# Reading the second input of VectorE's one-hot, bias and row-weighting instructions from PSUM instead of SBUF, in four graph passes and one attention stage of a graph network

## The reference

```python
def _hypergraph_conv(x, hei, W, b, num_nodes, num_edges):
    xw = x @ W.T
    edge_feat = b_inv[:, None] * segment_sum(xw[src], he)
    out = d_inv[:, None] * segment_sum(edge_feat[he], src)
    return out + b
...
logits = leaky_relu(s_dst[e0] + s_src[e1], 0.2)
m = segment_max(logits, e0)
ex = exp(logits - m[e0])
denom = segment_sum(ex, e0) + EPS
alpha = ex / denom[e0]
out = segment_sum(alpha[:, None] * h[e1], e0)
```

## Time and profile before

| what | value |
|---|---|
| median of 3 runs | 7260.24 us (7251.83 to 7262.59) |
| the profiled execution | 7256.75 us |
| its span | 7255.1 us |
| busy: PE, DVE, ACT, POOL | 4491.0, 2751.6, 961.2, 4754.5 us |
| POOL's gathers in s1 to s4 | from 137.9 us to 4546 us of the span |
| POOL's gathers in the attention | from 5461.3 us to 6693.3 us |

### The profile page before, as it was taken

One profiled execution on the slowest core, in us unless ns is written; L12 is line 12 of the kernel. 1 busy time (PEld: TensorE's weight loads), 2 busy tenths in 40 slices (PEclk: granted clock), 3 DMA queues, 4 the chain that ended last, 5 costly groups with the idle time before them and its releaser, 6 DMA issues. The chain is left out here.

```text
span 7255.1 us, 78015 instructions
## 1 busy us (share of the span) xinstructions
PE 4491.0 (62%) x18874; PEld 3567.0 (49%) x18874; DVE 2751.6 (38%) x7375; ACT 961.2 (13%) x2757; POOL 4754.5 (66%) x4610
## 2 busy tenths in 40 slices
PE   4565554666666555555556555899843656666589
PEld 3444443544554444444344444799632444444377
DVE  3111111222222111111454454322556666666644
ACT  2000000000111000000000000433330000000333
POOL 2777776777776777777777777111137777777455
PEclk8777777888888777877787888999876777777699
DMA  5888887333333333333444444052044444444445
GB/s 140 115 113 112 111 114 117 113 111 111 113 114 107 108 114 111 113 114 113 130 138 139 137 139 139 23 158 64 3 133 122 123 122 122 122 123 111 137 88 89
DMA packets 485564, 820.77 MB, mean 113 GB/s; under 512 B 108460, under 2 KB 344101, under 8 KB 485101
## 3 DMA queue, kind: packets, MB, share of 16 engines
q0 software_dynamic: 223760, 583.20, 36.2%
q1 hardware_dynamic: 261436, 232.51, 10.4%
q10 hardware_dynamic: 200, 3.43, 0.1%
HBM read 649.02 MB, written 170.02 MB: 113 GB/s over the span
## 5 line engine op out<-in xcount | busy, mean ns | idle before, releaser
L301 POOL DMA_INDIRECT s_rows<-table,ids x3328 | 3337.3, 1003 | 1111.3 <-issue 967.9
L554 PE MATMUL s_part<-s_rows,s_onehot 128*128 128x257 f32 x6656 | 2213.2, 498 | 1802.7 <-DMA s_rows<-table,ids 1774.3
L554 PEld LDWEIGHTS s_part<-s_rows,s_onehot 128*128 128x128 f32 x6656 | 1643.1, 256 | 2278.5 <-issue 1586.5
L1414 POOL DMA_INDIRECT at_rows<-h_t,ids x832 | 978.8, 1176 | 303.9 <-issue 252.0
L399 DVE TENSOR_SCALAR s_inv<-s_raw 128x1 f32<-128x1 f32 x416 | 64.0, 154 | 2857.7 <-ACT s_raw L348 2857.7
L1795 PE MATMUL at_part<-at_rows,at_onehot 128*128 128x264 f32 x1664 | 582.4, 484 | 4.9 <-DVE at_onehot L1622 4.9
L442 DVE TENSOR_TENSOR s_onehot<-iota,rel 128x1024 f32<-128x1024 f32 x416 | 510.5, 1228 | 63.6 <-DVE s_row L437 28.6
L348 ACT ACTIVATE s_raw<-s_part 128x257 f32<-128x257 f32 x416 | 161.0, 387 | 2443.3 <-PE s_part L554 2113.0
L1030 POOL COPY acc<-h 128x125 f32 x160 | 66.9, 418 | 557.7 <-DVE h L1058 557.7
L1795 PEld LDWEIGHTS at_part<-at_rows,at_onehot 128*128 128x128 f32 x1664 | 364.6, 237 | 70.8 <-issue 4.2
L2221 POOL DMA_INDIRECT out<-ex_y,ex_ids x112 | 181.1, 1617 | 162.2 <-DMA out<-ex_y,ex_ids 108.7
(11 more groups left out here) (355 smaller groups left out, 5612.6 us busy)
## 6 DMA issues: line engine op xcount, KB each, us to landing
s_rows<-table,ids POOLq DMA_INDIRECT x3328, 2.8
xs_d<-blank SPq DMA_DIRECT2D x38, 1032.0 KB, 12.7
table<-s_x SPq DMA_DIRECT2D x208, 128.0 KB, 2.6
ex_x<-xs_d SPq DMA_DIRECT2D x60, 258.0 KB, 3.3
table<-s_y SPq DMA_DIRECT2D x104, 128.0 KB, 1.9
s_at_node<-in_x SPq DMA_DIRECT2D x104, 128.0 KB, 2.8
s_at_node<-xn_d SPq DMA_DIRECT2D x104, 128.0 KB, 3.0
x_d<-s_x SPq DMA_DIRECT2D x104, 128.0 KB, 1.9
```

The source lines that it names most:

```text
L301: pool.indirect_dma_start(rows[:, t % RT, 0:D], None, table[0:NP_, :], bass.IndirectOffsetOnAxis(cst["ids"][:, t:t + 1], 0)).then_inc(rows ...
L554: ins = pe.matmul(part[u][:, 0:D + 1], onehot[:, u, t % JT, :], rows[:, t, 0:D + 1], start=False, stop=(t == JT * u + JT - 1))
L1414: pool.indirect_dma_start(rows[:, t % AHEAD, :], None, table, bass.IndirectOffsetOnAxis(cst["ids"][:, t:t + 1], 0)).then_inc(rows_in[t % A ...
```

## The change

Each stage gets one more PSUM bank (a second one in the attention), and a DVE copy at its start puts the column numbers there, and in the passes the bias behind them. The one-hots then read `iota` from PSUM and `rel` from SBUF; L410 reads `raw` from SBUF and the bias from PSUM. So that s2's banks suffice, its two `psY` become one, and `make` waits for one copy more.

In the attention the turned weights get a bank of their own, `ps_w`, and the row weighting reads them from there. That bank is single, so the weights of a round may be turned only when DVE has weighted the last tiles of the round before: the turn moves from step TIT + 2 to TIT + 5, with a wait on `weighted`, and the copy of the weights into the rows (still needed by PE, which sums them) moves from TIT + 3 to TIT + 6, with a semaphore of its own, `w_out`, on which DVE now waits at step 8.

```diff
+        fixed = m.ps(f"{name}_fixed", [P, 512])
+        iota = fixed[:, 0:P]
+        if bias is not None:
+            bias_row, bias = bias, fixed[:, P:P + D]
...
-            psY = [m.ps(f"{name}_psY{b}", [P, 512]) for b in range(2)]
+            psY = m.ps(f"{name}_psY", [P, 512])
...
+            dve.tensor_copy(iota, cst["iota"][:]).then_inc(held, 1)
+            if bias is not None:
+                dve.tensor_copy(bias, bias_row[:]).then_inc(held, 1)
+            dve.wait_ge(held, 1 if bias is None else 2)
...
-                link(dve.scalar_tensor_tensor(out=x[b][:], in0=raw[u][:, 0:D], scalar=inv[:, 0:1], in1=bias[:],
+                link(dve.scalar_tensor_tensor(out=x[b][:], in0=raw[u][:, 0:D], scalar=inv[:, 0:1], in1=bias,
...
-                dve.tensor_tensor(onehot[:, u % OG], cst["iota"][:].unsqueeze(1).to_broadcast([P, JT, P]),
+                dve.tensor_tensor(onehot[:, u % OG], iota.unsqueeze(1).to_broadcast([P, JT, P]),
...
-                pe.wait_ge(made_out, g + 1)
+                pe.wait_ge(made_out, g + 2)
...
+        ps_w = m.ps("at_ps_w", [P, 512])
+        iota = m.ps("at_iota", [P, 512])[:, 0:P]
...
+                if step == TIT + 6:
+                    act.wait_ge(w_turned, n + 1)
+                    act.sem_inc(issue, 1)
                     act.activation(rows[:, TIT * u:TIT * (u + 1), D:W],
-                                   ps_z[:, EXP:EXP + P].rearrange("p (t h) -> p t h", h=H8), ACT.Copy
-                                   ).then_inc(ex_ready, 1)
+                                   ps_w[:, 0:P].rearrange("p (t h) -> p t h", h=H8), ACT.Copy).then_inc(w_out, 1)
...
-                                      rv[:, :, D:W].unsqueeze(3).to_broadcast([P, G4, H8, D // H8]),
+                                      ps_w[:, t * H8:(t + G4) * H8].rearrange("p (t h) -> p t h", h=H8).unsqueeze(3)
+                                      .to_broadcast([P, G4, H8, D // H8]),
...
-                            dve.wait_ge(ex_ready, 3 * n + 7)
+                            dve.wait_ge(w_out, n + 2)
                             weigh_and_place(n + 1, (u + 1) % RB, t + JT - TIT)
...
-                    pe.transpose(ps_z[:, EXP:EXP + P], w[:], cst["ident"][:])
...
+                if step == TIT + 5:
+                    if not (isinstance(n, int) and n == 0):
+                        pe.wait_ge(weighted, TIT * n)
+                        pe.sem_inc(issue, 1)
+                        pe.wait_ge(w_out, n)
+                    pe.transpose(ps_w[:, 0:P], w[:], cst["ident"][:]).then_inc(w_turned, 1)
...
+                        if t == 0:
+                            pe.wait_ge(w_out, n + 1)
```

More of the change, by code:

```diff
@@ L240, in stage_row_pass @@
         summed, group_done, raw_ready = m.sem(f"{name}_summed"), m.sem(f"{name}_group_done"), m.sem(f"{name}_raw_ready")
+        held = m.sem(f"{name}_held")
         onehot_ready, cleared = m.sem(f"{name}_onehot_ready"), m.sem(f"{name}_cleared")
@@ L329, in copy_made @@
                 act.sem_inc(issue, 1)
-                act.activation(y[b][:], psY[b][:, 0:D], ACT.Copy).then_inc(made_out, 1)
+                act.activation(y[b][:], psY[:, 0:D], ACT.Copy).then_inc(made_out, 1)
             def round_of(i, opening):
@@ L374, in count_starts @@
                 dve.wait_ge(deg_turned, 2)
-                dve.tensor_copy(total[:], psY[0][:, 0:NB]).then_inc(deg_v, 1)
+                dve.tensor_copy(total[:], psY[:, 0:NB]).then_inc(deg_v, 1)
                 dve.wait_ge(deg_v, 3)
@@ L383, in count_starts @@
                 dve.wait_ge(deg_v, 6)
-                dve.tensor_tensor(cst["start"][:], upto[:], psY[1][:, 0:NB], ALU.add).then_inc(deg_v, 1)
+                dve.tensor_tensor(cst["start"][:], upto[:], psT[1][:, 0:NB], ALU.add).then_inc(deg_v, 1)
             def finish(g, u):
@@ L510, in count_starts @@
                 pe.wait_ge(deg_v, 1)
-                pe.matmul(psY[0][:, 0:NB], cst["ones"][:], deg[:], start=True, stop=True)
-                pe.matmul(psY[1][:, 0:NB], cst["before"][:], deg[:], start=True, stop=True).then_inc(deg_turned, 1)
+                pe.matmul(psY[:, 0:NB], cst["ones"][:], deg[:], start=True, stop=True)
+                pe.matmul(psT[1][:, 0:NB], cst["before"][:], deg[:], start=True, stop=True).then_inc(deg_turned, 1)
                 pe.wait_ge(deg_v, 7)
@@ L524, in make @@
                 pe.wait_ge(turned_out, g + 3)
-                pe.wait_ge(made_out, g + 1)
+                pe.wait_ge(made_out, g + 2)
                 for k in range(2):
-                    ins = pe.matmul(psY[b][:, 0:D], turned_x[b][:, k, :], w[:, k, :], start=(k == 0), stop=(k == 1))
+                    ins = pe.matmul(psY[:, 0:D], turned_x[b][:, k, :], w[:, k, :], start=(k == 0), stop=(k == 1))
                 ins.then_inc(made, 1)
@@ L1300, in stage_attention @@
         ps_line = m.ps("at_ps_line", [1, 2, 2, P])
-        EXP, INIT, FADE = P, 2 * P, 2 * P + 2
+        ps_w = m.ps("at_ps_w", [P, 512])
+        iota = m.ps("at_iota", [P, 512])[:, 0:P]
+        INIT, FADE = P, P + 2
         heads_in, node_in, starts_in = (m.sem(f"at_{n}") for n in ("heads_in", "node_in", "starts_in"))
@@ L1310, in stage_attention @@
         exped, ex_ready = m.sem("at_exped"), m.sem("at_ex_ready")
+        w_turned, w_out, held = m.sem("at_w_turned"), m.sem("at_w_out"), m.sem("at_held")
         prepared = m.sem("at_prepared")
@@ L1520, in _ @@
             fill()
+            dve.tensor_copy(iota, cst["iota"][:]).then_inc(held, 1)
+            dve.wait_ge(held, 1)
             dve.memset(carry[1][:], -BIG).then_inc(v, 1)
@@ L1610, in program @@
                     dve.wait_ge(added, 2)
-                dve.wait_ge(ex_ready, 4)
+                dve.wait_ge(w_out, 1)
                 def weigh_and_place(n, u, t):
@@ L1621, in weigh_and_place @@
                     rel = cst["rel"][:, int(not alone), :]
-                    dve.tensor_tensor(onehot[:, t:t + G4, :], cst["iota"][:].unsqueeze(1).to_broadcast([P, G4, P]),
+                    dve.tensor_tensor(onehot[:, t:t + G4, :], iota.unsqueeze(1).to_broadcast([P, G4, P]),
                                       rel[:, bass.ds(TIT * n + t, G4)].unsqueeze(2).to_broadcast([P, G4, P]),
@@ L1638, in collect @@
                         if left:
+                            dve.wait_ge(ex_ready, 2 * n + 5)
+                            dve.sem_inc(finishing, 1)
                             fades = factor[:, (u + 1) % RB, 2:2 + H8]
@@ L1659, in add_alone @@
                     if t == 0:
+                        dve.wait_ge(ex_ready, 2 * n + 3)
                         dve.wait_ge(added, TIT * n + 2)
@@ L1733, in prepare @@
                     pe.wait_ge(zc_ready, n + 1)
-                    pe.wait_ge(ex_ready, 3 * n + 1)
+                    pe.wait_ge(ex_ready, 2 * n + 1)
                     pe.transpose(ps_z[:, 0:P], zc[:], cst["ident"][:]).then_inc(pe_turned, 1)
```

## The result

The changed kernel takes **6942.69 us** (median of 4 runs, 6937.43 to 6949.73) where the kernel before takes 7258.40 on the same chip (4 runs): a ratio of 0.9566, 95% interval 0.9550 to 0.9583. The forecast of 6955 lies 12 us above it. The profiled execution took 6938.84 us, its span 6937.3, 317.8 us less than the span of before.

What follows compares the result with a forecast made beforehand. POOL's own gather rate was taken to bound passes and attention. 337.6 us removed, less 32 given back and 4 for the tie, gave 302 us: 7256.75 becomes 6954.9, forecast 6955, range 6920 to 7015.

Steps and rivals of the forecast that it cites:

- What bounds the kernel: Passes s1 to s4 and attention: nothing but POOL's own gather rate bounds these five stretches, 5.6 ms of 7.26.
- Removed, 337.6 us: Gathers' waits on POOL end: 159.7 us behind one-hots and 6.6 behind the bias in passes, 171.3 in the attention.
- Given back, 32 us: Passes and attention: freed gathers get caught by remaining DVE instructions with two SBUF inputs; 15 and 17 us, bounds 0 to 64.
- PSUM reads, 0.02 us each: DVE instructions reading PSUM take 0.02 us more each: 0.16 us a round in the attention, no cost in the passes.
- The rival price: DVE's PSUM reads cost 65 ns more by the skill's fixed cycles, making an attention round 0.5 us dearer instead of 0.16.
- the prediction's upper bound: Whole kernel: 7005 us, with 32 us more given back and the tie at 65 ns a PSUM read (18 us).
- The moved turn, 0.47 us a round on DVE's chain: Attention: the weights' turn, now before the `ps_line` turns DVE waits for, adds 0.47 us to DVE's chain each round.
- the new wait for `weighted`: Attention: PE's wait before turning the weights is already met when DVE does step 4, before it asks for the scores.
- The tie in the attention, 4 us: POOL and DVE each need 20.6 us a round, and two equal averages cost a little more: 4 us.
- The first rival: Attention becomes DVE's: its chain is 22 us a round, gain there 88 us instead of 151, total 7018 us; chance 0.12.
- The second rival: One-hots still keep gathers out, or lateness has another cause; no gain, 7257 to 7269 us; chance 0.04.
- The third: Attention: the weights' single bank holds DVE up 6.3 us a round or more; slower, such as 7335 us; chance 0.03.

Runs made afterwards that it cites:

- e1: Changed kernel with the attention's weights and the bias of s2 and s4 read from SBUF again, one-hots still from PSUM; 7817.63 us, 1.0002 of the kernel before.
- e2: Changed kernel with the one-hots' column numbers back in SBUF in all five stages, weights and bias from PSUM; 7834.64 us, 1.0030 of the kernel before.
- e8: The kernel before, unchanged, run beside the changed one on a chip taken for another than the result's; 7880.44 us, ratio 0.9992.
- e4: Changed kernel with PE's turn of the weights one step earlier, at TIT + 4, ahead of the scores' turn; 7835.04 us, 1.0025 of the kernel before.
- e3: Changed kernel with each one-hot of s1, s3 and the attention written twice, from PSUM, into a spare tile; 7856.69 us, 1.0066 of the kernel before.
- e9: The changed kernel as it is, run beside the kernel before on a chip taken for another than the result's; 7895.47 us, ratio 1.0018.
- e11: Changed kernel with PE's, DVE's and (but in s4) ACT's loops written out in passes and attention; 7847.03 us, 0.9949 of the kernel before.

## Why the prediction was right

*What bounds the kernel, and by how much.* Right, on the chip of the result. POOL's own rate set the five stretches, its idle time is unchanged to 0.3 us, and the stretches fell by 162.3 and 158.6 us where the sum had 151 and 151.

*Removed, 337.6 us.* Right. None of the 326, 45 and 199 waits is left; e1 and e2 bring them back one part at a time, e2 in the passes to 3357.0 us of gathers where the kernel before has 3359.2 (e8).

*Given back, 32 us.* The mechanism was right and its size a little too large. Measured against the plain prices of the forecast, 0.947 and 0.955 us, the passes keep 3174.8 - 3151.6 = 23 us (34 forecast), the attention 820.1 - 794.6 = 25.5 (30 forecast). s2 has 8.0 (7.5 forecast), s4 14.4 (22). In s4 58 gathers are late behind L426, 25 behind L424 and 29 behind L434, together 112 of 312 instructions, a little over the rate of one in three; but each is late by 0.13 us on average, not by half of 0.425. The phases of DVE's and POOL's rounds are not random to one another: the 29 behind L434, as long as the others, are late by 0.06 us on average. Some 5 us of the difference are no waits at all: the median itself fell from 947 to 946 and from 955 to 953 ns.

*PSUM reads, 0.02 us each.* Too high: medians of 672 ns for 682, 1225 for 1224, 1202 for 1216. The rival price, an estimate of 65 ns more from the cycles that the Trainium skill (VectorE: DVE Perf Modes, The TRN2 errata) has for PSUM to SBUF and for SBUF to SBUF, is not seen here at all in instructions of 512 and 1024 elements with one input in either memory. The product that the prediction's upper bound takes from it, 49 x 0.4, is 19.6 and not 18, which changes nothing.

*The moved turn, 0.47 us a round on DVE's chain.* Too high: 0.13. It was priced as if PE were always busy when the `ps_line` turn comes due, which may be why; e4 could not test it. The prediction has the new wait for `weighted` always met; it was not: PE's turn of the weights waited 11 times for DVE's L1632, 12.4 us in all and 1.6 at most. Nothing of it reached POOL, whose gaps stayed as they were.

*The tie in the attention, 4 us.* There was none. Both misprices went onto the same side: Without the wait for the scores, DVE's rounds come out at 19.6 us (forecast 20.6; 19.8 before by the same reckoning, the first two rounds left out), POOL's at 20.54 (forecast 20.6). The first rival, with its chance of 0.12, needed a chain of 22: it stayed 0.9 us under POOL's rounds and 2.4 under what that rival needed.

*The second rival,* that the one-hots would keep the gathers out, fell twice: by 401 gathers that read inside one, and by e3. With it falls what the Trainium skill (SBUF — State Buffer, Who interferes with whom) infers for tensor_tensor; its rule on two SBUF inputs is what the traces show, in e1 and e2 as in the result. The rule for at most one SBUF input has a condition there that the prediction leaves out, "outside the 2-port perf modes"; here gathers are late behind L413 and L425, with one, by up to 0.12 us. Whether these two run in such a mode no run shows. *The third,* the weights' single bank: 0.4 us of waiting in place of the 6.3 that it needs.

*Over the sum:* 321 us instead of 302, of which 11 in the passes and 4.5 in the attention were given back less, and 4 for the tie were not due.

What the forecast did not see is that the time it gives hangs on the chip. In so far it was luck that the result came from one on which the gathers set the time: on four others the same shorter gathers gave nothing. The profile of before shows gaps of 0.30 us without an exception in the passes; nothing in it says how far the next bound is when instructions are held up.

## What to carry to other kernels

Where POOL's indirect DMAs have a mean above their median, line up the late ones with DVE: if they end a fixed time behind instructions with both inputs in SBUF, move the operand that never changes (column numbers, a bias row), or the one that is in PSUM anyway, to PSUM; where the gathers set the time, it is worth the sum of their lateness, less what other such instructions then catch, and the order of the inputs does not matter. Where several instructions follow one another without a gap, the longest is worth most and the parts do not add. And before the gain is counted on, find the next bound: a wait on an engine that sets the time is worth its length only until another engine's delays end the same rounds.

## What was not expected of the hardware

- DVE reads one of two operands from PSUM at no cost: medians of 1225 against 1224 ns and 1202 against 1216 for 1024 elements, 672 against 682 for 512, 481 against 485 for the bias addition.
- An instruction with a single input tensor in SBUF (L413, L425, 353 ns) and a gather hold one another up, each in its own phase: DVE's up to 603 ns, the gather by up to 0.12 us.
- The same program takes 7258 us on one chip and 7817, 7821, 7883 and 7886 on four others, with the mean granted clock at 0.76 where the first has 0.80 (before) and 0.82 (after). The gathers are as long as on the first (medians of 946 to 949 ns in the passes). In spells PE starts one instruction per 0.7 or 1.4 us. A low clock is not what makes a spell: the one of e9 has 0.54 granted from 178 to 196 us, the one of e11 0.81 from 184 to 192.
- Scans with two SBUF inputs (L1569, L1587) hold gathers up like the elementwise instructions: 1.8 and 4.8 us over the attention of the changed kernel.
